# State-space scan: one VectorE scan instruction for two channel groups, batches written out, and the ends of a group placed between the scans of the next

## What is computed

```python
def step(state, xs):                       # over the 512 time steps
    d_t, B_t, C_t, u_t = xs
    dA = jnp.exp(d_t[..., None] * A)
    state = state * dA + (d_t * u_t)[..., None] * B_t[:, None, :]
    return (state, jnp.einsum('ben,bn->be', state, C_t))
y = (y + D * u) * silu(z)                  # z is the layer norm of x
x = x + tanh(g_xattn[2]) * swapaxes(y, 1, 2)
```

## Time and profile before

| what | value |
|---|---|
| median of 3 runs | 3627.48 us (3620.82 to 3627.97) |
| profiled execution | 3628.22 us |
| its span, first to last instruction | 3626.5 us |
| busy share of the span | PE 71%, PEld 33%, DVE 64%, ACT 43%, POOL 32% |
| mean granted TensorE clock | 0.855 of full speed |
| state-space scan stage | from 1477.7 us to 2014.1 us of the span |

### The profile page before, as it was taken

How to read it: one execution, slowest core, us unless ns; L and a number is a source line. 1 busy time by engine, 2 the same in 40 slices (tenths; PEclk the granted TensorE clock), 3 DMA queues, 4 the chain that set the end, 5 groups by cost and what they waited for, 6 DMA issues and landing times. The chain is left out here.

```text
span 3626.5 us, 45547 instructions
## 1 busy us (share of the span) xinstructions
PE 2570.6 (71%) x14044; PEld 1190.2 (33%) x14044; DVE 2336.5 (64%) x4043; ACT 1569.0 (43%) x2159; POOL 1169.2 (32%) x958
## 2 busy tenths in 40 slices
PE   3987998799564554367657389972978888748991
PEld 1432333343221221012112267751522222424660
DVE  6665663556546344789889756656568887555664
ACT  3534552443221144444444155542546677113870
POOL 5756661000001111567667122215650000001434
PEclk9979999799575676699889689996979999869995
DMA  3541301110000000000000177753642100212995
GB/s 132 192 157 47 103 13 59 50 35 12 3 0 9 19 0 0 1 1 0 0 0 0 47 238 241 242 157 111 218 134 71 48 13 13 90 39 82 323 311 164
DMA packets 162839, 305.96 MB, mean 84 GB/s; under 512 B 33299, under 2 KB 80671, under 8 KB 160246
## 3 DMA queue, kind: packets, MB, share of 16 engines
q1 hardware_dynamic: 139462, 223.49, 17.7%
q0 software_dynamic: 23216, 80.49, 7.8%
HBM read 210.34 MB, written 93.32 MB: 84 GB/s over the span
## 5 line engine op out<-in xcount | busy, mean ns | idle before, releaser
L2060 DVE TENSOR_REDUCE ac_nmax<-ac_M 128x1 f32<-128x512 f32 (+1 forms) x768 | 497.1, 687 | 152.5 <-PE ac_M L1874 147.9
L2038 ACT ACTIVATE ac_PT<-ac_S 128x1024 f32<-128x1024 f32 x384 | 371.2, 1017 | 160.8 <-PE ac_S L1909 142.4
L2806 PE MATMUL sc_y<-sc_hc,ident 128*128 128x512 f32 x512 | 293.3, 657 | 141.8 <-POOL sc_hc L2782 140.6
L2782 POOL TENSOR_TENSOR sc_hc<-sc_h,sc_cs 128x512 f32<-128x512 f32 x256 | 324.3, 1267 | 173.8 <-DVE sc_h L2884 171.2
L2884 DVE TENSOR_TENSOR_SCAN sc_h<-sc_dA,sc_dB 128x512 f32<-128x512 f32 x256 | 310.2, 1213 | 9.7 <-ACT sc_dA L2844 9.7
L2844 ACT ACTIVATE sc_dA<-sc_dl,sc_A 128x512 f32<-128x512 f32 x256 | 176.4, 690 | 176.8 <-DVE sc_h L2884 176.8
L2806 PEld LDWEIGHTS sc_y<-sc_hc,ident 128*128 128x128 f32 x512 | 79.3, 193 | 333.8 <-POOL sc_hc L2782 331.0
L2458 POOL TENSOR_TENSOR f_o<-f_o,f_bias 128x512 f16<-128x512 f32 x16 | 20.6, 1289 | 519.9 <-DVE f_o L2507 519.9
L2876 DVE TENSOR_TENSOR sc_dB<-ss_du,sc_b 128x512 f32<-128x512 f32 x256 | 168.7, 660 | 15.8 <-PE sc_b L2796 15.8
L1874 PE MATMUL ac_M<-KT,QT 64*128 64x512 f16 (+1 forms) x384 | 140.9, 428 | 41.0 <-DVE ac_nmax L2060 23.8
L813 POOL DMA_INDIRECT mo_g<-normalised,mo_cur x112 | 146.0, 1304 | 61.3 <-POOL mo_cur L809 44.2
(11 more groups left out here) (498 smaller groups left out, 6120.9 us busy)
## 6 DMA issues: line engine op xcount, KB each, us to landing
slot_results<-mo_o SPq DMA_DIRECT2D x56, 512.0 KB
mo_up<-in_w_gate SPq DMA_DIRECT2D x24, 704.0 KB, 5.4
mo_up<-in_w_up SPq DMA_DIRECT2D x24, 704.0 KB, 6.8
keys_t<-ap_kto SPq DMA_DIRECT2D x32, 512.0 KB, 2.7
queries_t<-ap_qto SPq DMA_DIRECT2D x32, 512.0 KB, 2.6
mo_up<-in_exp_up SPq DMA_DIRECT2D x32, 512.0 KB
mo_dn<-in_exp_down SPq DMA_DIRECT2D x32, 512.0 KB
mo_dn<-in_w_down SPq DMA_DIRECT2D x24, 512.0 KB
```

The source lines that it names most:

```text
L2038: nc.scalar.activation(PT[:, n % PTB, :, :], psS[:, 2 * (n % 2):2 * (n % 2) + 2, :], ACT.Exp, scale=SCALE / (SQK * SQK)).then_inc(exp_done, 1)
L2060: last = v.tensor_reduce(out[:, :, 0], sc[:, 0:MAIN], AX.X, ALU.max)
L2782: nc.gpsimd.tensor_tensor(hc[:, m % RC, :], h[:, m % RH, :], cs[:, n % 2, :], ALU.mult).then_inc(hc_done, 1)
L2806: nc.tensor.matmul(py[:, c, :], env.id32[:], hc[:, m % RC, :], start=(n == 0), stop=(n == NS - 1)).then_inc(y_mm, 1)
```

## The change

A unit becomes one state of a **pair** of channel groups (W = 2), 1024 columns: 32 units a batch in two groups of 16 (NG = 8 groups `gp`), 128 units in all. Decay, input, state and `hc` are held for both halves side by side, `dA` in four PSUM banks (2 buffers of 2 x 512). One scan instruction runs over both halves; column 0 of each half of `dA` is set to zero once, and `exp` writes columns 1 to 511 only, so the state is started anew there. The rows of B and C are made once for each unit, so twice as often as before. `Fori` over batches is written out, and `bc` and `delta` are read where they lie, without the copies. `z` is no longer made on DVE: `silu` takes the norm's scale and shift (`gates`, four ACTIVATEs, after unit 8 of each batch). `py` holds one group; at the end of a group the work on it stands between the scans of the next: `collect` after scan 1, `gate` after `hc` 1, `turned` on PE before the first sum, `update` after scan 3. Rings: `RB, RH, RC = 2, 3, 3`.

```diff
-    NU = NS * KD
-    RA, RB, RH, RC = 2, 3, 4, 3
+    W = 2
+    NP = KD // W
+    NG = B * NP
+    NU = NG * NS
+    RB, RH, RC = 2, 3, 3
...
+        py = ps("y", [P, W, S])
+        pb, pc, dA = ps("b", [P, S]), ps("c", [P, S]), ps("dA", [P, 2, W, S])
...
         @block.gpsimd
...
+            for m in range(NU):
+                gp, b, p, n = unit(m)
+                pool.wait_ge(c_ev, m + 1)
+                pool.wait_ge(h_done, m + 1)
+                if m >= RC:
+                    pool.wait_ge(y_mm, m - RC + 1)
+                nc.gpsimd.tensor_tensor(hc[:, m % RC, :, :], h[:, m % RH, :, :],
+                                        cs[:, m % 2, :].unsqueeze(1).to_broadcast([P, W, S]), ALU.mult
+                                        ).then_inc(hc_done, 1)
+                if gp and n == 1:
+                    gate(gp - 1)
+            gate(NG - 1)
...
         @block.tensor
...
+            def b_row(m):
+                gp, b, p, n = unit(m)
+                if m:
+                    pe.wait_ge(dB_done, m)
+                nc.tensor.matmul(pb[:], sel[:, n, :], bc[:, b, :], start=True, stop=True).then_inc(b_mm, 1)
+
+            def c_row(m):
+                gp, b, p, n = unit(m)
+                if m:
+                    pe.wait_ge(c_ev, m)
+                nc.tensor.matmul(pc[:], sel[:, NS + n, :], bc[:, b, :], start=True, stop=True).then_inc(c_mm, 1)
...
+            def turned(gp):
+                pe.wait_ge(yg_done, gp + 1)
...
+                last.then_inc(yt_done, 1)
+                pe.wait_ge(x_done, gp + 1)
+
+            def summed(m):
+                gp, b, p, n = unit(m)
+                pe.wait_ge(hc_done, m + 1)
+                for c in range(W):
+                    last = nc.tensor.matmul(py[:, c, :], env.id32[:], hc[:, m % RC, c, :], start=(n == 0),
+                                            stop=(n == NS - 1))
+                last.then_inc(y_mm, 1)
...
+            rows(0)
+            rows(1)
+            for gp in range(NG):
+                m = gp * NS
+                for n in (2, 3, 4):
+                    rows(m + n)
+                if gp:
+                    turned(gp - 1)
+                summed(m)
+                rows(m + 5)
+                summed(m + 1)
+                summed(m + 2)
+                rows(m + 6)
+                summed(m + 3)
+                summed(m + 4)
+                for n in range(5, NS):
+                    rows(m + n + 2)
+                    summed(m + n)
+            turned(NG - 1)
...
         @block.scalar
...
+            for m in range(NU):
+                gp, b, p, n = unit(m)
+                if m >= 2:
+                    act.wait_ge(h_done, m - 1)
+                for c in range(W):
+                    k = p * W + c
+                    last = nc.scalar.activation(dA[:, m % 2, c, 1:S], delta[:, b * KD + k, 1:S], ACT.Exp, scale=A[:, k, n:n + 1])
+                last.then_inc(dA_done, 1)
+                act.wait_ge(c_mm, m + 1)
+                if m >= 2:
+                    act.wait_ge(hc_done, m - 1)
+                nc.scalar.activation(cs[:, m % 2, :], pc[:], ACT.Copy).then_inc(c_ev, 1)
+                if p == 0 and n == NS // 2:
...
+                    gates(b)
...
         @block.vector
         def _(dve):
             ch = Chain(dve, own)
+            nc.vector.memset(dA[:, :, :, 0:1], 0.0).then_inc(cleared, 1)
...
+            nc.vector.scalar_tensor_tensor(out=shift[:], in0=agg[:, :, 0], scalar=-1.0, in1=rstd[:], op0=ALU.mult,
+                                           op1=ALU.mult).then_inc(shift_done, 1)
+
+            def inputs(m):
+                gp, b, p, n = unit(m)
+                dve.wait_ge(b_mm, m + 1)
+                if m >= RB:
+                    dve.wait_ge(h_done, m - RB + 1)
+                nc.vector.tensor_tensor(dB[:, m % RB, :, :], chans(du, b, p), pb[:].unsqueeze(1).to_broadcast([P, W, S]),
+                                        ALU.mult).then_inc(dB_done, 1)
+
+            def scan(m):
+                dve.wait_ge(dB_done, m + 1)
+                dve.wait_ge(dA_done, m + 1)
+                if m >= RH:
+                    dve.wait_ge(hc_done, m - RH + 1)
...
+            inputs(0)
+            for m in range(NU):
+                gp, b, p, n = unit(m)
+                if m + 1 < NU:
+                    inputs(m + 1)
+                scan(m)
+                if gp and n == 1:
+                    collect(gp - 1)
+                if gp and n == 3:
+                    update(gp - 1)
+            collect(NG - 1)
+            update(NG - 1)
```

More of the change, by code:

```diff
@@ L2772, in _, with gate @@
                 pool.wait_ge(sel_done, i + 2)
[L2773 to L2787, removed]
+            def gate(gp):
+                b, p = divmod(gp, NP)
+                pool.wait_ge(g_done, b + 1)
+                pool.wait_ge(y_ev, gp + 1)
+                nc.gpsimd.tensor_tensor(yt[:], yt[:], g[:, p * W:(p + 1) * W, :], ALU.mult).then_inc(yg_done, 1)
+            for m in range(NU):
[10 more added lines that the diff above has]
+            gate(NG - 1)
         @block.tensor
@@ L2826, in _ @@
             act.wait_ge(a_done, 2)
[L2827 to L2855, removed]
+            act.wait_ge(cleared, 1)
@@ L2864, in _ @@
             ch.link(nc.vector.reciprocal(rstd[:], rstd[:]))
[L2865 to L2897, removed]
-                    nc.vector.tensor_tensor(yt[:, c % 2, :], py[:, c, :], at(u, b * KD + c), ALU.add).then_inc(y_ev, 1)
-                    if c:
-                        update(dve, b, c - 1)
-                update(dve, b, KD - 1)
-                dve.wait_ge(x_done, (b + 1) * KD)
@@ new lines, in collect, with update @@
+            def collect(gp):
+                b, p = divmod(gp, NP)
+                dve.wait_ge(y_mm, (gp + 1) * NS)
+                nc.vector.tensor_tensor(yt[:], py[:], chans(u, b, p), ALU.add).then_inc(y_ev, 1)
+            def update(gp):
+                b, p = divmod(gp, NP)
+                dve.wait_ge(yt_done, gp + 1)
+                for c in range(W):
+                    k = p * W + c
+                    xv = env.x[:, b * TPB:(b + 1) * TPB, k * P:(k + 1) * P]
+                    last = nc.vector.scalar_tensor_tensor(out=xv, in0=py[:, c, :].rearrange("p (t e) -> p t e", e=P),
+                                                          scalar=env.th[:, 2:3], in1=xv, op0=ALU.mult, op1=ALU.add)
+                last.then_inc(x_done, 1)
```

70 lines of the change are left out of this document (33 added, 37 removed).

## The result

| | before | changed |
|---|---|---|
| median | 3627.72 us (3620.82 to 3628.43, 4 runs) | 3695.01 us (3689.09 to 3701.34, 4 runs) |
| profiled execution | 3628.22 us | 3695.94 us |
| ratio to before | | 1.019, 95% interval 1.0169 to 1.0211 |
| scan stage, first scan to end of last update | 514.0 us | 589.3 us |
| mean granted TensorE clock | 0.855 | 0.846 |

The change makes the kernel 67 us slower; the forecast was 3685 us. The profiled executions differ by 67.7 us: the stage from its first scan on is 75.3 us longer, the first scan comes 6.1 us sooner after the stage's beginning, and 1.4 us were won ahead of the stage, where nothing was changed.

A forecast was written before the change was run, and what follows sets the result against it. PE's written order was taken to bound the changed scan stage: 553.6 us for groups and tail, plus 24 for the clock, less 514.0 before and 5.5 at the start, gives +58 us, or 3685 us, range 3600 to 3730.

The forecast's parts named there:

- PE's written order closes a loop: Inside a group, the row of B stands behind a waiting sum: 8.23 us for two units, where DVE needs 3.31 each.
- Prices: Instructions on 1024 columns: scan 2.20, dB 1.11, hc 2.36 us; a pair costs DVE 3.31 in place of 3.43.
- rival 2: Scan stage: DVE stays the bound at 3.31 us a unit, so the kernel gets faster, 3593 us; chance 17%.
- Ends of a group: Work on a finished group delays the next: scan 3 ends at 16.2 us, scan 4 starts at 21.2; 68.7 a group.
- Clock at the ends: TensorE's clock falls at every new group end, so the first two sums run slower: 24 us in all.
- The term of 24 us: Seven group ends at 3.4 us: summed(0) and summed(1) each 1.71 us longer at the lower clock.
- rival 3: The clock falls inside groups as well: some 3800 to 3820 us, or 3730 if in half the units; chance 13%.
- main case: Scan stage: PE's loop at 4.12 us a unit plus clock falls at group ends: 3685 us, alone 3670 to 3705; 44%.
- gates hidden, start 5.5 us earlier: ACT's four pauses of 5.0 us are covered by slowed DVE, otherwise 2 us each; the first scan starts 5.5 us earlier.
- First group and tail: The first group, with no end before it, takes about 61 us; work after the last scan takes 11.6.
- 88 us of edges: In the faster rival, 66 of the 88 us at batch edges, where DVE mostly waits, would go.
- fetching the written-out code costs nothing: Instruction fetch for the written-out code was taken as 0, since each instruction lasts over a microsecond.

The follow-up runs named there:

- e1: The changed kernel with PE's rows of B and C three units ahead of the sum in place of two: 3645.67 us, ratio 1.006.
- e3: The changed kernel with rows three units ahead and three buffers of dB in place of two: 3633.31 us, ratio 1.0022.
- e9: e6 with rows of B three units ahead of the sum, C two, and unit 5's row of B before a group's first sum: 3589.82 us.
- e6: e3 with group ends started one scan earlier, and gates moved between the decay and the copy of C: 3601.97 us, ratio 0.9927.
- e2: The changed kernel with only a third buffer of dB added: 3689.62 us, ratio 1.0181.
- e8: e6 with each unit's fused scan split into two instructions of 512 columns: 3608.73 us, ratio 0.9956.

## Why the prediction was right, and what in it was not

The sign, the mechanism and the size held: 58 us forecast, 67 measured.

- **PE's written order closes a loop.** Right, and shown: 8.20 us measured for two units against 8.23; one unit more of lead took 49 us off (e1), the falls of the clock inside the groups among them.
- **Prices.** `hc` 2.353 (2.36 taken), scan 2.18 to 2.20 where it isn't held (2.20), `dB` 1.11 to 1.14 (1.11). What was missed is a wait: in units 0 to 3 a unit is 3.53 and not 3.31, because two buffers of `dB` make `inputs` wait for the scan ahead of it. It is off the loop of the changed kernel, so it cost it little. But rival 2 was priced without it: with DVE as the bound and this ring the unit is 3.53, *longer* than the 3.43 of two old units. The fused scan and the ring together lose 0.1 us a unit; only with the third buffer does the fusing win.
- **Ends of a group.** The schedule held: `collect` after scan 1, gap of scan 3 to 4 of 9.0 us, against 7.2 with the clock up and 8.9 with `summed(0)` at the lower one.
- **Clock at the ends.** It fell at every end, as said. The term of 24 us was the one mis-sized: it counted `summed(1)` in full, but the scans after the gap stand 3.9 to 4.8 apart, since the rows were ahead there. Measured against the schedule: about 1.8 us for each of seven ends, 13 in all.
- **Clock inside the groups.** This was rival 3, given 13%, and it came true in part beside the main case. Group 4 lasts 69.7 us without such a fall; groups 1, 2, 3, 5 and 6 are 4.5, 7.9, 3.1, 4.7 and 2.8 us longer, 23 together, and the last group about 5 more (its first fourteen distances against those of group 4). So the near hit of the total is in part luck: errors of both signs stand in it. The forecast stage was 577.6 us (553.6 and 24), the measured one 589.3. Of the difference, 11 us were too much for the clock at the ends and 28 are missing inside the groups; the rest of group 4 is 0.8 shorter than its schedule, 6 us over seven groups, the last scan follows the one before it after 2.2 and not 4.1 us, and the first group and the tail are 1.5 and 2.0 longer, together the 12 us. The main case should have been the loop with both kinds of fall. The argument used against the rival (dense work at the lower clock lets it rise) fits the trace, where the falls inside the groups are short; it did not prevent the next.

  What the Trainium skill says of bursts with waits between them ("TensorE: Matmul & The Clock Gate", HAM oscillation) agrees with this trace in the repetition, though not in every burst: the clock fell at 1588.7, 1605.8 and 1622.9 us in group 1, behind waits of 1.92, 2.25 and 2.24 us, but not behind the one of 3.04 at 1614.2.
- **gates hidden, start 5.5 us earlier.** Right: no wait for the decay over 0.2 us, and the first scan 6.1 us earlier. The cover of `gates` was DVE's own slowness, as said; e1 took it away and the pause cost 4.5 us each, 5.7 to 5.8 in e3 (forecast: 2). Part of it was PE's row of C, which stood ahead of a sum and waited for ScalarE: with it one unit later, in e9, a pause costs 1.1 us in place of the 3.3 to 3.6 of e6.
- **First group and tail.** 62.5 against 61: scan 3 to 4 already takes 4.39 us, with a wait of 0.97 for a row of B while the clock is still at 0.5. It is not the ring, since e2's first group is only 0.2 shorter. The tail takes 13.6 against 11.6 (last sums and turning at the lower clock).
- **Rival 2 (faster).** Edges were there to be had, but not with this order. The rival's 88 us of edges count four; the stage of before holds three of 22 and a tail of 9.7. e9's stage is 35 us shorter than before: 15 of these are the shorter unit (3.31 for 3.43), about 20 are edges.

  The sentence of the Trainium skill on grouping ("Perfetto Trace Analysis", Optimizing Scalar/DVE Operations) holds here and is worth 0.05 us a unit for the scan (e8). Its other sentence, on breaking up what causes bubbles elsewhere, named the danger; here an earlier row sufficed, and no instruction had to be broken up (breaking up the product or the sums was not tried).

That fetching the written-out code costs nothing is contradicted by no trace. The changed kernel's profile shows six waits of POOL with no releaser, 15.5 us together and up to 4.0 at once, but each is ahead of the product of unit 1 of a group and ends 0.13 us after the scan that this product reads, as ordinary products do:

```profile
1636.86 2.28 DVE L2918 TENSOR_TENSOR_SCAN sc_h<-sc_dA,sc_dB 128x1024 f32<-128x1024 f32 x1
...
1639.28 2.36 POOL L2795 TENSOR_TENSOR sc_hc<-sc_h,sc_cs 128x1024 f32<-128x1024 f32 x1 [3.57 <-issue]
```

In e1, which is written out as well, there is none. Open: what decides whether the clock falls inside a group. It is not the length of the last wait alone, as the 3.04 us without a fall show.

## What to carry to other kernels

When work units are made larger, every chain between engines gets longer while the distance, in units, at which a helper runs ahead stays the same: write out the loop from one unit to the one that needs its helper, add up start-to-start times and divide by the units it spans; if that exceeds the bound engine's time per unit, order the helper further ahead before anything else. A ring one buffer short costs even on a single engine, and pauses hidden under a slow engine reappear when it is mended. Fusing two scans into one on a saturated engine earned 0.2% here. Against the changed kernel, one unit more of lead gave 49 us, the third buffer of `dB` 12, shorter ends 24, the earlier `gates` 7 and the rows of B and C ordered apart 12; only with these together is the kernel 1% faster than before.

## What was not expected of the hardware

The clock falls inside steady work, and the mean share of work does not decide it. With distances alternating 3.99 and 4.21 us it stayed at 1.00 (group 4); with 3.53 and 4.67 us, the same mean and the same work, it fell repeatedly (groups 1, 2 and 5). The bunched rhythm gathers PE's idle time, 3.36 us a pair in both, into one large piece. The timeline of PE in the changed kernel shows a pair of sums in group 1, the second with a fall in it, and a pair in group 4 (in brackets the idle time before them):

```profile
1617.75 1.98 PE L2831 MATMUL sc_y<-sc_hc,ident 128*128 128x512 f32 x4 [1.12 <-POOL sc_hc L2795]
...
1622.40 3.41 PE L2831 MATMUL sc_y<-sc_hc,ident 128*128 128x512 f32 x4 [2.24 <-POOL sc_hc L2795]
...
1835.29 1.98 PE L2831 MATMUL sc_y<-sc_hc,ident 128*128 128x512 f32 x4 [1.79 <-POOL sc_hc L2795]
...
1839.27 1.98 PE L2831 MATMUL sc_y<-sc_hc,ident 128*128 128x512 f32 x4 [1.57 <-POOL sc_hc L2795]
```

That the bunching causes the falls is argued and not shown. In every group that has them, the 3.53 and 4.67 begin only behind a first fall, so the fall may as well make the rhythm. In group 3 the first fall came out of a nearly even rhythm of 3.87 and 4.33 us, behind a wait of 1.91 us (second line below), while group 4 had the same wait in the same rhythm without a fall (last two lines). The first line, from group 1, has the longer wait of 3.04 us without a fall:

```profile
1614.21 1.98 PE L2831 MATMUL sc_y<-sc_hc,ident 128*128 128x512 f32 x4 [3.04 <-POOL sc_hc L2795]
...
1751.25 2.56 PE L2831 MATMUL sc_y<-sc_hc,ident 128*128 128x512 f32 x4 [1.91 <-POOL sc_hc L2795]
...
1810.34 1.98 PE L2831 MATMUL sc_y<-sc_hc,ident 128*128 128x512 f32 x4 [1.45 <-POOL sc_hc L2795]
...
1814.68 1.98 PE L2831 MATMUL sc_y<-sc_hc,ident 128*128 128x512 f32 x4 [1.92 <-POOL sc_hc L2795]
```

And a second 512-column scan behind the first costs 0.05 us more than the same columns in one instruction.
